# A feed-forward pipeline's token shift, moved to another place in GpSimd's order

## The chip, the cores and the metric

The kernel runs on one core of a Trainium2 chip. The metric is the device time of one execution in microseconds (us), the median of the runs shown. The engines are TensorE (PE in the profile), VectorE (DVE), ScalarE (ACT), GpSimd (POOL) and the DMA queues; each works through its own list of instructions in order, and they meet only at semaphores.

## The reference, cut to what matters

The whole program runs two blocks on 16 sequences of 256 tokens, 128 wide: a linear attention, a mixture of experts, a retention layer, and last a stack of two layers of local attention and a gated feed-forward part. The change touches only the feed-forward parts of those two layers:

```python
def shift_token(t):
    t1, t2 = jnp.split(t, 2, axis=-1)
    t2 = jnp.pad(t2, ((0, 0), (1, 0), (0, 0)))[:, :-1]
    return jnp.concatenate([t1, t2], axis=-1)

# in _layer, after the attention:
h = shift_token(x)
mu = h.mean(-1, keepdims=True)
var = h.var(-1, keepdims=True)
h = (h - mu) / jnp.sqrt(var + 1e-05) * lg + lb
h = h @ w1 + b1                       # 128 -> 2 x 341
a, g = jnp.split(h, 2, axis=-1)
h = a * jax.nn.gelu(g, approximate=False)
x = x + h @ w2 + b2                   # 341 -> 128
```

The shift takes the second half of the features from the token before, within each sequence.

## The kernel before, in words

The 4096 tokens are 8 chunks of 512 columns (`CH`), with the 128 features on the partitions. The feed-forward part works on pairs of chunks (`W = 2`, `PAIRS = 4`); within a pair the chunks are i = 0 and i = 1. The 341 hidden units are three blocks (`NHB`), j = 0, 1, 2, of 128, 128 and 85 rows. Each of the two layers has one such part, and a layer's part starts when the attention before it is done and ends before the next one's work.

One chunk goes through this chain:

1. GpSimd copies the chunk into `hs[i]` (`hsf` in the profile), the first 64 rows as they are and the other 64 moved by one token (`shift`, lines 2172 and 2173).
2. TensorE multiplies by the matrix that subtracts the mean (`centre`, L2216); ScalarE squares (L2270); TensorE averages the squares (`variance`, L2224); ScalarE takes logarithm and exponential for 1/sqrt (`roots`, L2276 and L2278).
3. VectorE multiplies, scales, and rounds to a high part (`inputs`, L2322, L2324, L2327). GpSimd subtracts to make the low part (`low_inputs`, L2181).
4. TensorE makes both halves of the hidden units from three products high*high, low*high, high*low (`hidden_units`, L2236); ScalarE applies gelu (L2286); VectorE multiplies with the other half (`units`, L2333).
5. The high part of the units comes from VectorE for chunk 0 (L2341) and from ScalarE for chunk 1 (L2295), the low part from GpSimd, three blocks of each chunk (`low_units`, L2190).
6. TensorE makes the output, nine matmuls for a chunk (`output`, L2248), and VectorE adds it to the residual stream `k.H` (L2346).

There is no planner: every engine has a loop over steps written by hand, and its order is the order of its queue. In a step s, TensorE works on three pairs at once:

```python
for step in range(PAIRS + 2):
    if step < PAIRS:
        centre(step)
    if step > 1:
        output(step - 2, 0)
    if step < PAIRS:
        variance(step)
    if step > 1:
        output(step - 2, 1)
    if 0 < step <= PAIRS:
        hidden_units(step - 1)
```

`centre(pair)` waits for each chunk's shift by the semaphore `shifted`. `output(pair, i)` waits for all low units of its chunk by `u_lo`. `hidden_units` waits for `hn_lo`. ScalarE loads the table for logarithm and exponential, does the squares and roots of pair s, loads the gelu table and does the gelus of pair s - 1. VectorE does the residual of pair s - 2 around the inputs of pair s, and then the units of pair s - 1.

GpSimd shifts pair 0 before its loop. In step s it then shifts pair s + 1, makes the low inputs of pair s, and the low units of pair s - 1. The shift has one pair of buffers `hs[0]`, `hs[1]`, which `centre` must have read before they are written again.

Of the kernel before, what the change touches and what calls it, by code (L numbers as in the profile page):

```python
# [8 lines left out]
F32 = mybir.dt.float32  # L9
BF16 = mybir.dt.bfloat16  # L10
F32R = mybir.dt.float32r
ALU = mybir.AluOpType
# [39 lines left out]
def hid_rows(j):  # L52
    return min(P, HID - j * P)


NHB = (HID + P - 1) // P
# [1590 lines left out]
def later(a):  # L1647

    return a.rearrange("p (s t) -> p s t", t=SEQ)[:, :, 1:SEQ]


def shifted_views(k, cols):

    return k.H[0:DH, cols], k.H[DH:P, cols].rearrange("p (s t) -> p s t", t=SEQ)[:, :, 0:SEQ - 1]
# [20 lines left out]
def local_layer(k, l, shared):  # L1675
# [4 lines left out]
    nc, ps = k.nc, k.ps  # L1680
    with ExitStack() as big:
# [5 lines left out]
        with ExitStack() as ctx:  # L1687
# [8 lines left out]
            W = k.sb(f"W{l}", [P, RING, CH], ctx=ctx)  # L1696
# [36 lines left out]
            @block.sync  # L1733
            def _(sp):
                for n in names:
                    sp.dma_start(w[n][:], k.dram[n][l]).then_inc(w_in, 16)
                if raw:
                    prepare_loads(k, l + 1, raw, sp)
# [404 lines left out]
        with ExitStack() as ctx:  # L2143
            W = 2
            PAIRS = NCH // W
# [3 lines left out]
            U = k.sb(f"Uf{l}", [P, W, NHB, CH], ctx=ctx)  # L2149
            U_parts = [k.sb(f"Uf_{part}{l}", [P, W, NHB, CH], F32R, ctx) for part in ("hi", "lo")]  # L2150
# [7 lines left out]
            first = lambda pair: G0 + W * pair  # L2158
            block = ctx.enter_context(nc.Block())

            @block.gpsimd
            def _(pool):

                def shift(pair):
                    if pair > 1:
                        pool.wait_ge(hn_lo, first(pair - 1))
                    for i in range(W):
                        c = first(pair) + i
                        early, late = shifted_views(k, here(c))
                        if pair > 0:  # L2170
                            pool.wait_ge(centred, c - 1)
                        nc.gpsimd.tensor_copy(hs[i][0:DH, :], early).then_inc(shifted, 1)
                        nc.gpsimd.tensor_copy(later(hs[i][DH:P, :]), late).then_inc(shifted, 1)
                    pool.wait_ge(shifted, 2 * (c + 1) + W * L)

                def low_inputs(pair):
                    for i in range(W):
                        c = first(pair) + i
                        hi, lo = (part[i] for part in hn_parts[pair % 2])
                        pool.wait_ge(hn_hi, c + 1)  # L2180
                        nc.gpsimd.tensor_tensor(lo[:], hn[i][:], hi[:].bitcast(F32), ALU.subtract).then_inc(hn_lo, 1)  # L2181

                def low_units(pair):
                    for i in range(W):
                        for j in range(NHB):
                            n = hid_rows(j)
                            if j == 0 and (i or pair):
                                pool.wait_ge(u_lo, NHB * (first(pair) + i))
                            pool.wait_ge((u_hi_dve, u_hi_act)[i], NHB * (first(pair) // W) + j + 1)
                            nc.gpsimd.tensor_tensor(U_parts[1][0:n, i, j, :], U[0:n, i, j, :],  # L2190
                                                    U_parts[0][0:n, i, j, :].bitcast(F32), ALU.subtract).then_inc(u_lo, 1)

                for i in range(W):
                    nc.gpsimd.memset(hs[i][:], 0.0).then_inc(shifted, 1)
                pool.wait_ge(shifted, 2 * G0 + W * L)
                shift(0)
                for step in range(PAIRS + 1):
                    if step > 1:
                        pool.wait_ge(u_lo, NHB * first(step - 1))
                    if step + 1 < PAIRS:  # L2200
                        shift(step + 1)
                    if step < PAIRS:
                        low_inputs(step)
                    if step > 0:
                        low_units(step - 1)

            @block.tensor
            def _(pe):
# [286 lines left out]
```

## Time and profile before

| | |
|---|---|
| time, median of 3 runs | 1434.64 us (1432.21 to 1435.32) |
| the profiled execution's own time | 1433.24 us |
| its span, first to last instruction | 1431.4 us |
| PE busy | 1210.3 us (85%) |
| DVE busy | 1043.1 us (73%) |
| ACT busy | 883.9 us (62%) |
| POOL busy | 844.3 us (59%) |
| mean granted TensorE clock | 0.941 of full |

The two feed-forward parts lie at about 970 to 1053 us and 1336 to 1420 us of the span. A timeline gives for each entry the start, the length, the engine, the line, the output and inputs by their names in the program, and in square brackets how long the engine had been idle before it and on what it had waited. A merged entry (x4) has the length of the whole group. A matmul of 32-bit floats with 512 columns shows as two entries of one line, so the two chunks of `centre` are an entry of x4. Entries of matmuls overlap their successors, because their ends are modelled.

### The profile page before, as it was taken

The numbers are of one execution on the slowest core, as the hardware profiler recorded it, in microseconds if no ns is written. First come the engines' busy times: TensorE is split into PE (matmuls) and PEld (weight loads), VectorE is DVE, ScalarE is ACT, GpSimd is POOL, SyncE is SP. The second block draws the span as 40 slices with busy tenths as digits, with TensorE's granted clock in tenths as the row PEclk, the third lists the DMA queues.
The fourth block names the chain that finished last, engine by engine and source line by source line (L and its number), as shares of the span: only waits on it lengthen the run. The fifth ranks groups of instructions, "written<-read, shape, count | busy, mean of one in ns | idle before, by whom it ended". The sixth has DMA issues, their size and how long they took to land. (4 is left out here: it accounts for less than half of the span.)

```text
span 1431.4 us, 26528 instructions
## 1 busy us (share of the span) xinstructions
PE 1210.3 (85%) x7852; PEld 787.8 (55%) x7852; DVE 1043.1 (73%) x2573; ACT 883.9 (62%) x2302; POOL 844.3 (59%) x778
## 2 busy tenths in 40 slices
PE   6879999963869997597699999966968999999796
PEld 3333344323548885242477777753645777777464
DVE  1289998975888996465688888843648888887464
ACT  6623333322536663176599899955648889899564
POOL 0054444505753667411688888877558887887663
PEclk9899999985989999699899999998979999999999
DMA  4800000002330221400100000000000000000001
GB/s 113 280 1 0 0 0 1 0 1 81 106 113 27 89 70 37 150 1 2 52 2 3 1 0 1 0 1 0 1 23 2 3 3 1 1 0 1 1 1 59
DMA packets 35021, 43.99 MB, mean 31 GB/s; under 512 B 5620, under 2 KB 24977, under 8 KB 34912
## 3 DMA queue, kind: packets, MB, share of 16 engines
q1 hardware_dynamic: 30304, 34.27, 7.5%
q0 software_dynamic: 4608, 8.47, 1.9%
q8 instruction: 43, 0.70, 0.2%
q14 instruction: 66, 0.54, 0.1%
HBM read 22.65 MB, written 21.12 MB: 31 GB/s over the span
## 5 line engine op out<-in xcount | busy, mean ns | idle before, releaser
L2066 DVE TENSOR_TENSOR R<-bank,tab 128x1024 f32<-128x1024 f32 x128 | 156.1, 1224 | 78.1 <-ACT sq L1976 77.1
L2010 ACT ACTIVATE W<-W,nm 128x128 f32<-128x128 f32 x512 | 198.2, 393 | 0.4
L1763 POOL TENSOR_TENSOR R<-R 128x512 f32<-128x512 f32 x128 | 161.3, 1282 | 15.1 <-DVE R L2066 15.1
L1778 POOL TENSOR_TENSOR W<-W,rden 128x512 f32<-128x512 f32 x128 | 132.8, 1040 | 50.5 <-DVE rden L2096 45.5
L2089 DVE CUSTOM_DVE_ANT_0 W<-bank,mask_q,rn 128x128 f32<-128x128 f32 x512 | 147.4, 344 | 17.7 <-PE bank L1878 13.1
L1308 POOL DMA_INDIRECT expert_rows<-Yt,xin x80 | 82.5, 1032 | 68.0 <-DVE Yt L1281 50.0
L1011 POOL DMA_INDIRECT expert_slots<-tok_rows,dst x64 | 67.2, 1050 | 65.9 <-ACT tok_rows L1035 45.1
L2010 ACT ACTIVATION_READ_ACCUMULATOR W<-W,nm 128x1 f32 x512 | 98.7, 193 | 0.0
L1994 ACT ACTIVATE QK<-bank 128x512 f32<-128x512 f32 x128 | 74.9, 586 | 35.2 <-PE bank L1853 33.5
L726 DVE TENSOR_TENSOR_SCAN S<-beta,U 128x512 f32<-128x512 f32 x64 | 93.5, 1482 | 0.0
L1903 PE MATMUL bank<-PT,VA 128*64 128x128 f32 (+1 forms) x1024 | 86.2, 262 | 3.7 <-ACT PT L2018 2.8
L1878 PE MATMUL bank<-QK 64*64 64x128 f32 x2048 | 86.3, 284 | 3.3 <-DVE nm L2089 3.0
L1976 ACT ACTIVATE sq<-bank 128x512 f32<-128x512 f32 x128 | 74.5, 582 | 19.0 <-PE bank L1832 18.3
L1772 POOL TENSOR_TENSOR R<-R,rn 128x512 f32<-128x512 f32 x64 | 66.7, 1042 | 28.9 <-ACT rn L1984 25.4
L1832 PE MATMUL bank<-wqkv_hi,hs_hi 128*128 128x512 f32 x128 | 64.2, 501 | 18.2 <-POOL hs_lo L1751 12.7
L2018 ACT ACTIVATE PT<-bank 128x512 f32<-128x512 f32 x128 | 74.8, 589 | 6.6 <-PE bank L1888 6.6
L2190 POOL TENSOR_TENSOR Uf_lo<-Uf,Uf_hi 128x512 fp32r<-128x512 f32 (+1 forms) x48 | 61.1, 1285 | 26.9 <-DVE Uf_hi L2341 26.2
L2073 DVE TENSOR_REDUCE sums<-sq 128x16 f32<-128x1024 f32 x64 | 76.8, 1201 | 0.0
L1888 PE MATMUL bank<-ident,W 128*128 128x128 f32 x512 | 75.7, 273 | 0.0
L1903 PEld LDWEIGHTS bank<-PT,VA 128*64 128x64 f32 x1024 | 52.2, 138 | 40.9 <-issue 40.8
L1888 PEld LDWEIGHTS bank<-ident,W 128*128 128x128 f32 x512 | 62.6, 140 | 15.9 <-issue 0.7
L1878 PEld LDWEIGHTS bank<-QK 64*64 64x64 f32 x2048 | 55.4, 133 | 20.9 <-issue 16.9
(350 smaller groups left out, 3475.9 us busy)
## 6 DMA issues: line engine op xcount, KB each, us to landing
expert_slots<-empty SPq DMA_DIRECT2D x8, 650.0 KB, 6.5
xin<-expert_slots SPq DMA_DIRECT2D x8, 650.0 KB, 6.1
expert_rows<-empty SPq DMA_DIRECT2D x8, 512.0 KB, 6.7
pair_rows<-expert_rows SPq DMA_DIRECT2D x16, 256.0 KB, 4.5
expert_raw<-w1e_dram SPq DMA_DIRECT2D x9, 256.0 KB, 2.9
expert_raw<-w2e_dram SPq DMA_DIRECT2D x9, 256.0 KB, 3.1
tok<-x_dram SPq DMA_DIRECT2D x8, 256.0 KB, 4.7
out_dram<-tok_out SPq DMA_DIRECT2D x8, 256.0 KB, 3.2
```

The source lines that it names most:

```text
L726: nc.vector.tensor_tensor_scan(S[i][:], beta[i % 2][:, chunk(c)], U[i // 2][:], 0.0, ALU.mult, ALU.add).then_inc(s_scan, 1)
L1308: nc.gpsimd.indirect_dma_start(k.ys[:, :], bass.IndirectOffsetOnAxis(ap=ids, axis=0), Yt[:, s % 3, t, :], None, bounds_check=2 * T - 1, oo ...
L1763: nc.gpsimd.tensor_tensor(halves[:, :, 0, :, z, :], halves[:, :, 0, :, z, :], halves[:, :, 1, :, 1 - z, :], ALU.add).then_inc(summed, 1)
L1778: nc.gpsimd.tensor_tensor(x, x, scale.to_broadcast([P, 4, P]), ALU.mult).then_inc(scaled, 1)
L1878: m = nc.tensor.matmul(ps[BS[i]][r:r + WIN, blk // 2 * P:(blk // 2 + 1) * P], QK[par][rows, b, o:o + WIN], keys, start=True, stop=True)
L1888: m = nc.tensor.transpose(ps[BT[p % 2]][:, a * P:(a + 1) * P], W[:, p % RING, a * P:(a + 1) * P], k.const["ident"][:])
L1903: m = nc.tensor.matmul(ps[BO[p % 2]][i * DH:(i + 1) * DH, cols], v[:, 2 * b + i, :], PT[:, p % 2, i * SEQ + cols.start:i * SEQ + cols.stop ...
L1994: nc.scalar.activation(QK[par][:, qk * NB:(qk + 1) * NB, t * P:(t + 1) * P], ps[BX[(t + 1) % 2]][:].rearrange("p (a b) -> p a b", a=NB), A ...
L2010: m = nc.scalar.activation(x, x, ACT.Exp, scale=-1.0, bias=nm[:, p % RING, j:j + 1], accum_out=den[:, p % RING, j:j + 1])
L2066: nc.vector.tensor_tensor(R[:, i, qk, :, :].rearrange("p c (h d) -> p c h d", d=DH), x, y.to_broadcast([P, 2, HEADS, DH]), ALU.mult).then_ ...
L2073: nc.vector.tensor_reduce(sums[:, i, :, 0:1].rearrange("p h o -> p (h o)"), sq[:].rearrange("p q (h d) -> p (q h) d", d=DH), AX.X, ALU.add ...
L2089: m = nc.vector.tensor_tensor_reduce(W[:, p % RING, j * P:(j + 1) * P], ps[BS[i]][:, cols], k.const["mask_q"][:, cols], rn[:, par, 2 * s + ...
```

## The change

GpSimd's order within a step is altered. `low_units` does one chunk at a time; the shift of the next pair no longer opens the step, but stands between the low units of the two chunks. In step 0, in which there are no low units, it follows the low inputs. Its waits on GpSimd's own earlier work (`hn_lo`, `u_lo`) are set to the new place. No instruction is added or taken away apart from waits, and the other engines' code is the same.

```diff
                 def shift(pair):
+                    if pair > 0:
+                        pool.wait_ge(hn_lo, first(pair))
                     if pair > 1:
-                        pool.wait_ge(hn_lo, first(pair - 1))
+                        pool.wait_ge(u_lo, NHB * (first(pair - 2) + 1))
                     for i in range(W):
...
-                def low_units(pair):
-                    for i in range(W):
-                        for j in range(NHB):
-                            n = hid_rows(j)
-                            if j == 0 and (i or pair):
-                                pool.wait_ge(u_lo, NHB * (first(pair) + i))
-                            pool.wait_ge((u_hi_dve, u_hi_act)[i], NHB * (first(pair) // W) + j + 1)
-                            nc.gpsimd.tensor_tensor(...).then_inc(u_lo, 1)
+                def low_units(pair, i):
+                    for j in range(NHB):
+                        n = hid_rows(j)
+                        if j == 0 and (i or pair):
+                            pool.wait_ge(u_lo, NHB * (first(pair) + i))
+                        pool.wait_ge((u_hi_dve, u_hi_act)[i], NHB * (first(pair) // W) + j + 1)
+                        nc.gpsimd.tensor_tensor(...).then_inc(u_lo, 1)
...
                 for step in range(PAIRS + 1):
                     if step > 1:
                         pool.wait_ge(u_lo, NHB * first(step - 1))
-                    if step + 1 < PAIRS:
-                        shift(step + 1)
                     if step < PAIRS:
                         low_inputs(step)
                     if step > 0:
-                        low_units(step - 1)
+                        low_units(step - 1, 0)
+                    if step + 1 < PAIRS:
+                        shift(step + 1)
+                    if step > 0:
+                        low_units(step - 1, 1)
```

## Rows read from the trace of the kernel before

**Rows 1.** Busy time in the two feed-forward parts; columns: engines, clock, DMA share, GB/s.

```profile
970.00:1053.00 83.00, 69.51 (x248) 44.41 (x248) 44.53 (x69) 48.53 (x69) 51.80 (x50) 0.96 0.00 1
1336.00:1420.00 84.00, 70.16 (x248) 44.43 (x248) 44.51 (x68) 48.42 (x68) 51.92 (x51) 0.96 0.00 1
```

**Rows 2.** Waits in the first layer's part: total us, times, longest.

```profile
PE bank L2248 <- POOL Uf_lo L2190: 3.7, 4, 1.5
```

**Rows 3.** Timeline of GpSimd in the first layer's part.

```profile
971.73 0.61 POOL L2173 COPY hsf<-H 64x510 f32<-64x510 f32 x1
...
974.60 0.61 POOL L2172 COPY hsf<-H 64x512 f32<-64x512 f32 x1 [0.94 <-PE bank L2216]
...
982.64 1.27 POOL L2181 TENSOR_TENSOR hnf_lo<-hnf,hnf_hi 128x512 fp32r<-128x512 f32 x1 [0.82 <-PE bank L2216]
983.98 0.60 POOL L2172 COPY hsf<-H 64x512 f32<-64x512 f32 x1
...
987.29 1.29 POOL L2181 TENSOR_TENSOR hnf_lo<-hnf,hnf_hi 128x512 fp32r<-128x512 f32 x1 [0.43 <-DVE hnf_hi L2327]
...
994.59 5.14 POOL L2190 TENSOR_TENSOR Uf_lo<-Uf,Uf_hi 85x512 fp32r<-85x512 f32 x4 [0.36 <-DVE Uf_hi L2341]
999.80 0.60 POOL L2172 COPY hsf<-H 64x512 f32<-64x512 f32 x1
...
1001.80 0.61 POOL L2173 COPY hsf<-H 64x510 f32<-64x510 f32 x1
1003.83 1.29 POOL L2181 TENSOR_TENSOR hnf_lo<-hnf,hnf_hi 128x512 fp32r<-128x512 f32 x1 [1.42 <-DVE hnf_hi L2327]
...
1012.05 5.12 POOL L2190 TENSOR_TENSOR Uf_lo<-Uf,Uf_hi 85x512 fp32r<-85x512 f32 x4 [0.36 <-DVE Uf_hi L2341]
```

**Rows 4.** Timeline of TensorE and ScalarE in the same part.

```profile
972.39 3.78 PE L2216 MATMUL bank<-hsf,centre 128*128 128x512 f32 x4 [13.68 <-POOL hsf L2173]
...
978.12 1.10 PE L2224 MATMUL bank<-sqf,mean 128*128 128x512 f32 x2 [0.87 <-ACT rsf L2276]
...
979.51 1.10 PE L2216 MATMUL bank<-hsf,centre 128*128 128x512 f32 x2 [0.29 <-DVE hnf L2322]
...
982.57 1.12 PE L2224 MATMUL bank<-sqf,mean 128*128 128x512 f32 x2
...
984.56 1.10 PE L2224 MATMUL bank<-sqf,mean 128*128 128x512 f32 x2 [0.87 <-ACT rsf L2276]
...
995.70 1.88 PE L2216 MATMUL bank<-hsf,centre 128*128 128x512 f32 x4
...
997.01 0.80 PE L2248 MATMUL bank<-Uf_hi,w2f_hi 128*128 128x512 f32 x1
...
998.71 1.09 ACT L2270 ACTIVATE sqf<-bank 128x512 f32<-128x512 f32 x2
...
999.51 1.02 PE L2224 MATMUL bank<-sqf,mean 128*128 128x512 f32 x2
...
1012.90 1.88 PE L2216 MATMUL bank<-hsf,centre 128*128 128x512 f32 x4
```

**Rows 5.** Timeline of TensorE at the next attention's start and the second layer's part.

```profile
1057.49 0.79 PE L1832 MATMUL bank<-wqkv_hi,hs_hi 128*128 128x512 f32 x1 [5.67 <-POOL hs_lo L1751]
...
1338.99 3.78 PE L2216 MATMUL bank<-hsf,centre 128*128 128x512 f32 x4 [3.75 <-POOL hsf L2173]
...
1345.35 1.10 PE L2224 MATMUL bank<-sqf,mean 128*128 128x512 f32 x2 [0.87 <-ACT rsf L2276]
```

**Rows 6.** Stretches after those two idle times, columns as in rows 1.

```profile
1055.00:1060.00 5.00, 2.51 (x6) 1.82 (x6) 0.20 (x1) 1.06 (x2) 2.31 (x2) 0.50 0.27 102
1338.00:1345.00 7.00, 5.49 (x6) 1.77 (x6) 0.00 (x0) 1.68 (x3) 4.53 (x8) 0.52 0.00 0
```

**Rows 7.** Timeline of VectorE: the same operation beside an idle and a busy GpSimd.

```profile
979.40 0.55 DVE L2324 TENSOR_SCALAR hnf<-hnf,vec 128x512 f32<-128x512 f32 x1
...
987.81 1.05 DVE L2324 TENSOR_SCALAR hnf<-hnf,vec 128x512 f32<-128x512 f32 x1
```

More of the change, by code:

```diff
@@ L2181, in low_inputs @@
                         nc.gpsimd.tensor_tensor(lo[:], hn[i][:], hi[:].bitcast(F32), ALU.subtract).then_inc(hn_lo, 1)
-                def low_units(pair):
-                    for i in range(W):
-                        for j in range(NHB):
-                            n = hid_rows(j)
-                            if j == 0 and (i or pair):
-                                pool.wait_ge(u_lo, NHB * (first(pair) + i))
-                            pool.wait_ge((u_hi_dve, u_hi_act)[i], NHB * (first(pair) // W) + j + 1)
-                            nc.gpsimd.tensor_tensor(U_parts[1][0:n, i, j, :], U[0:n, i, j, :],
-                                                    U_parts[0][0:n, i, j, :].bitcast(F32), ALU.subtract).then_inc(u_lo, 1)
+                def low_units(pair, i):
[4 more added lines that the diff above has]
+                        pool.wait_ge((u_hi_dve, u_hi_act)[i], NHB * (first(pair) // W) + j + 1)
+                        nc.gpsimd.tensor_tensor(U_parts[1][0:n, i, j, :], U[0:n, i, j, :],
+                                                U_parts[0][0:n, i, j, :].bitcast(F32), ALU.subtract).then_inc(u_lo, 1)
                 for i in range(W):
```

## The prediction, made before the changed kernel ran

> **What bounds the kernel now.** I read the page first. Its chain of work that ended last covers only the final output and says nothing of the stage that changes, so the answer must come from that stage. The busy times by window show two feed-forward parts of 83 and 84 us, TensorE busy 69.5 and 70.2 us of them, GpSimd only 51.8 [rows 1]. TensorE is the engine nearest to the bound, and in program order it holds the dependency chain of all three pairs in flight. Each part is a serial stretch: the attention before it must be done, and the next one needs its residual. So a microsecond lost on TensorE's order there is lost from the run.
>
> The list of waits shows TensorE waiting for GpSimd's low units four times, 3.7 us in all [rows 2]; those are in the last steps, where no shift stands in the queue, so the change cannot take them away. What matters is the timeline of GpSimd around each shift, beside TensorE's time of first use.
>
> - The shift of pair 1 is made at 974.60, as soon as `centre` has released the buffers, in a stretch in which GpSimd has nothing else to do until the first low inputs [rows 3]. TensorE uses it at 979.51, when its bank comes free [rows 4].
> - The shift of pair 2 starts at 983.98. After it GpSimd is still idle for 0.43 us until the high inputs of pair 1 come from VectorE [rows 3].
> - The shift of pair 3 starts at 999.80, and 1.42 us of idle time follow it, again until high inputs come [rows 3].
>
> So none of the three shifts delays the low inputs behind it: each lies in idle time. And each is ready long before TensorE wants it: `centre` of pair 2 runs at 995.70, that of pair 3 at 1012.90, both with no wait [rows 4]. A shift that costs nothing now can only be moved to a place where it costs something or nothing.
>
> **The change part by part.** A shift is four copies: from the start of the first (999.80) to the start of the fourth (1001.80) are 2.00 us, so one copy each 0.67, the first chunk ready after 0.67 + 0.61 = 1.28 and the second after 2.61 [rows 3]. TensorE starts 0.05 us after a shift is ready (971.73 + 0.61 = 972.34, then 972.39) [rows 3, 4]. GpSimd goes from one operation to a dependent one in 0.07 (982.64 + 1.27 = 983.91, then 983.98); that row already is a shift behind low inputs with a wait on the engine's own semaphore, so the altered waits on `hn_lo` and `u_lo` add nothing [rows 3].
>
> *Step 0, pair 1's shift.* There are no low units yet, so it stands behind the low inputs of pair 0, which end at 983.91 because they need the whole chain of pair 0. It starts at 983.98 instead of 974.60, and TensorE starts `centre` of chunk 0 at 983.98 + 1.28 + 0.05 = 985.31 instead of 979.51, of chunk 1 at 986.64. Queued behind `centre` on TensorE are `variance` of pair 1 and then all hidden units of pair 0, whose inputs have long been ready. What counts is when the second `variance` starts, for hidden units follow it at once; before, that is 984.56 [rows 4]. At full clock: an entry of four matmuls takes 1.88, four passes of about 0.43, so TensorE can start the first `variance` 0.87 after the second `centre`, at 987.51; the second follows 1.99 later (982.57 to 984.56) [rows 4], at 989.50. That is 4.9 us late.
>
> TensorE's last work before is at 978.12 + 1.10 = 979.22 [rows 4], so it would now stand idle for 6.1 us. The trace has two near rows: after 5.67 us of idle time the granted clock is 0.50 (1.2 GHz), and after 3.75 us it is 0.52 in the next 7 us [rows 5, 6]. With half clock the same sequence, two `centre` and two `variance` whose shifts arrive 1.3 us apart, can be read at the two starts: from first `centre` to second `variance` 978.12 - 972.39 = 5.73 us in layer 0 and 1345.35 - 1338.99 = 6.36 us in layer 1 [rows 4, 5]. Then the second `variance` is at 985.31 + 5.73 to 6.36 = 991.0 to 991.7, which is 6.5 to 7.1 us late. I take 6.8, the middle, for the idle times of 3.75 and 5.67 us are shorter than 6.1 and still ended in half clock [rows 5, 6], and after the longer one, 13.68 us, four matmuls took 3.78 us instead of 1.88 [rows 4].
>
> The Trainium skill, in "TensorE: Matmul & The Clock Gate", section on HAM oscillation, says that a pause of TensorE between bursts makes the next burst start at half rate, and that this is paid at each such pause. By that rule step 0 costs 6.8 us; with the clock kept it would cost 4.9. The rows agree with the rule.
>
> *Step 1, pair 2's shift.* From here on all is late by the same amount, so I reckon with the old times. The last low units of chunk 0 start at 994.59; the entry of four takes 5.14, one 1.285 [rows 3]. They end at 995.88, the shift starts at 995.95, and `centre` runs its chunk 0 at 997.28 and chunk 1 at 995.95 + 2.61 + 0.05 = 998.61. Before, chunk 1 ran two passes after 995.70, at 996.57 [rows 4]. So TensorE is 2.05 us late behind it. ScalarE does not cover this: its squares start at 998.71 because of the table load [rows 4], but between `centre` and `variance` TensorE has the nine matmuls of `output` (997.01 to 999.51) [rows 4], which start behind chunk 1's `centre` and run gapless into `variance`. All 2.05 us reach `variance`, and from there roots, inputs and the hidden units of pair 1.
>
> *Step 1, low units of chunk 1.* They are behind the shift, so they end at 995.88 + 2.65 + 3 * 1.285 = 1002.4 instead of 999.73. The `output` that needs them starts at about 999.51 + 2.05 + 2.4 = 1004.0, so nothing waits. GpSimd is free for pair 2's low inputs at 1002.5, and these come at 1003.83 + 2.05. Cost nothing; the cover is 1.6 us on TensorE's side.
>
> *Step 2, pair 3's shift.* The same with 1012.05: ready for chunk 1 at 1012.05 + 1.285 + 0.07 + 2.61 + 0.05 = 1016.07 instead of 1012.90 + 0.87 = 1013.77 [rows 3, 4]. 2.30 us late.
>
> *Steps 3 and 4* have no shift and keep their lengths.
>
> *What is gained.* While GpSimd copies, a VectorE operation of pair 1 takes 1.05 us instead of 0.55 [rows 7]. That shift is no longer beside it. But gelu is needed by the next VectorE work at nearly the same time, so I take 0 and at most 0.5 us a part. The Trainium skill, "GPSIMD Engine Reference", section on specifications, says that the two engines share their interfaces to SBUF and get in each other's way; the rows agree, and by it alone this change would save that half microsecond.
>
> *The sum.* Per layer 6.8 + 2.05 + 2.3 = 11.15 us, for both 22.3. Layer 1's part has the same order and the same length [rows 1]. 1433.24 + 22.3 = 1455.5 us. The profiled execution was 1.4 below the median of the runs; half of that is within their scatter, so I say 1456.
>
> **The rivals.**
>
> *A. The clock does not fall.* Layers cost 4.9 + 2.05 + 2.3 = 9.25 each: 1433.24 + 18.5 = 1451.7. Against it stand the three idle times above.
>
> *B. The clock stays low through hidden units.* The attention after 1057.49 is still at 0.50 well into its matmuls [rows 6]. Pair 0's first twelve hidden matmuls would then take double: nine gapless ones take 2.50 us (997.01 to 999.51) [rows 4], so twelve take 3.3 and would take 3.3 more, part of it beside the load of the gelu table. In both layers up to 1433.24 + 22.3 + 6.6 = 1462.1, and 1458.8 if half of it shows.
>
> *C. No change.* The late shifts would have to be hidden by TensorE's own waits. For it: TensorE waits 0.87 us for ScalarE ahead of each second `variance` [rows 4]. Against: those waits follow the late work and move with it. Time 1434.
>
> *D. Faster.* The shift at the head of steps 1 and 2 holds GpSimd for 2.7 us ahead of low inputs. If these were the real bound, through a wait that the profile puts elsewhere, four shifts (two a layer) would give 4 * 2.7 = 10.8: 1422.4. It decides only if low inputs became ready before the shift was over; the idle 0.43 and 1.42 us behind the shifts say that they did not [rows 3].
>
> **How the numbers follow.** Forecast 0.66, A 0.12, B 0.14, C 0.05, D 0.03. Bounds within the forecast: clock rows 6.47 and 7.10, the gain of 0 to 0.5 a part, the scatter of the runs of 1.5: 1453 to 1458. With A and B the range is 1450 to 1461. What can be told from no change is 0.2%, 2.9 us: slower 0.92, same 0.05, faster 0.03.
>
> **What the profile after would show.** GpSimd's timeline: in step 0 low inputs first, then copies; TensorE idle about 6 us before the second pair's `centre`, put down to the copy L2173; a granted clock of 0.5 right after; waits on L2173 of about 1.5 and 0.5 us before `centre` of pair 2, and 1.8 and 0.5 before that of pair 3; parts of about 94 and 95 us; everything outside them as before. The prediction is wrong if the first `variance` of pair 1 is not late, or if the parts keep 83 us.

## The result, and the profile after

The changed kernel takes 1457.85 us (median of 4 runs, 1456.21 to 1462.35), the kernel before 1434.98 us in the same comparison (1432.21 to 1437.57): ratio 1.0163, 95% interval 1.0143 to 1.0182. It is slower by 22.9 us; the forecast was 1456.0 us, range 1450 to 1461.

The profiled execution of the changed kernel took 1457.24 us, its span is 1455.4 us, 24.0 more than before. Busy times of VectorE, ScalarE and GpSimd are those of before within 1.2 us. TensorE has 7.7 us more with the same 7852 matmuls. All of it lies in the two feed-forward parts (72.4 and 75.0 us instead of 69.5 and 70.2), where the granted clock is 0.93 and 0.89 instead of 0.96 [rows 1]: the same work, more of it at the lower clock. The busy times of the whole execution:

```profile
PE 1218.0 (84%) x7852; PEld 790.3 (54%) x7852; DVE 1043.4 (72%) x2573; ACT 884.7 (61%) x2302; POOL 843.1 (58%) x778
```

The list of waits of the first feed-forward part has the one group that grew on TensorE: it waits for the shift's second copy (now L2175) 23.4 us in six waits, where before it did so once, for 13.7 us, at the part's start. The waits for low units are the same 3.7 us as in [rows 2]:

```profile
PE bank L2219 <- POOL hsf L2175: 23.4, 6, 13.7
...
PE bank L2251 <- POOL Uf_lo L2191: 3.7, 4, 1.5
```

GpSimd's timeline shows the three shifts in their new places, in answer to [rows 3]. The first stands behind the low inputs of pair 0, with 7.21 us of idle time behind it; the other two, of which the first is shown, stand behind the third low unit of chunk 0, with the three of chunk 1 right behind them:

```profile
982.85 1.26 POOL L2183 TENSOR_TENSOR hnf_lo<-hnf,hnf_hi 128x512 fp32r<-128x512 f32 x1 [0.82 <-DVE hnf_hi L2330]
984.18 0.60 POOL L2174 COPY hsf<-H 64x512 f32<-64x512 f32 x1
...
986.17 0.61 POOL L2175 COPY hsf<-H 64x510 f32<-64x510 f32 x1
993.99 1.29 POOL L2183 TENSOR_TENSOR hnf_lo<-hnf,hnf_hi 128x512 fp32r<-128x512 f32 x1 [7.21 <-DVE hnf_hi L2330]
...
1001.52 1.29 POOL L2191 TENSOR_TENSOR Uf_lo<-Uf,Uf_hi 85x512 fp32r<-85x512 f32 x1 [0.36 <-DVE Uf_hi L2344]
1002.93 0.60 POOL L2174 COPY hsf<-H 64x512 f32<-64x512 f32 x1
...
1004.92 0.61 POOL L2175 COPY hsf<-H 64x510 f32<-64x510 f32 x1
1005.62 3.76 POOL L2191 TENSOR_TENSOR Uf_lo<-Uf,Uf_hi 128x512 fp32r<-128x512 f32 x3
1012.97 1.29 POOL L2183 TENSOR_TENSOR hnf_lo<-hnf,hnf_hi 128x512 fp32r<-128x512 f32 x1 [3.60 <-DVE hnf_hi L2330]
```

TensorE's timeline, in answer to [rows 4]: `centre` (now L2219) waits 6.08 us in step 1 of TensorE, 1.47 + 0.21 in the next, 1.71 + 0.21 in the one after. The rows from 1005.59 to 1008.65 show how `output` and the first `variance` follow the second `centre` without a gap, so a late `centre` is a late `variance`:

```profile
978.33 1.10 PE L2227 MATMUL bank<-sqf,mean 128*128 128x512 f32 x2 [0.87 <-ACT rsf L2279]
985.50 3.78 PE L2219 MATMUL bank<-hsf,centre 128*128 128x512 f32 x4 [6.08 <-POOL hsf L2175]
989.08 1.62 PE L2227 MATMUL bank<-sqf,mean 128*128 128x512 f32 x2
991.56 1.10 PE L2227 MATMUL bank<-sqf,mean 128*128 128x512 f32 x2 [0.87 <-ACT rsf L2279]
...
1004.26 1.12 PE L2219 MATMUL bank<-hsf,centre 128*128 128x512 f32 x2 [1.47 <-POOL hsf L2175]
1005.59 1.12 PE L2219 MATMUL bank<-hsf,centre 128*128 128x512 f32 x2 [0.21 <-POOL hsf L2175]
1006.15 0.80 PE L2251 MATMUL bank<-Uf_hi,w2f_hi 128*128 128x512 f32 x1
...
1008.65 1.02 PE L2227 MATMUL bank<-sqf,mean 128*128 128x512 f32 x2
...
1023.93 1.13 PE L2219 MATMUL bank<-hsf,centre 128*128 128x512 f32 x2 [1.71 <-POOL hsf L2175]
```

The busy times by window of the same stretch: in the idle stretch TensorE does nothing, and in the 6.5 us behind it the granted clock is 0.63 on average, that is, mostly the 1.2 GHz level. The matmuls of 985.50 took 3.78 us, the same as the cold four in [rows 4].

```profile
979.50:985.40 5.90, 0.00 (x0) 0.00 (x0) 2.90 (x6) 2.56 (x3) 3.69 (x4) 0.83 0.00 1
985.50:992.00 6.50, 5.63 (x7) 2.05 (x8) 0.00 (x0) 2.43 (x4) 1.22 (x2) 0.63 0.00 0
```

**Where the time went, part by part.** The start of the first part moves by several us from run to run for reasons outside it, so the experiments below are read by the parts' own lengths in the profiled execution: from the start of the first copy of the shift to the start of the last residual on VectorE.

| kernel | first part, us | second part, us | more than before |
|---|---|---|---|
| before | 80.79 | 81.47 | |
| changed | 92.10 | 94.67 | 11.31 + 13.20 |
| e1_step0_back | 85.33 | 87.66 | 4.54 + 6.19 |
| e2_only_step0 | 88.13 | 88.45 | 7.34 + 6.98 |
| e3_kept_busy | 90.71 | 90.95 | 9.92 + 9.48 |
| e4_shift_last | 96.77 | 96.06 | 15.98 + 14.59 |
| e5_after_low_inputs | 80.78 | 81.63 | -0.01 + 0.16 |
| e6_last_low_on_dve | 80.19 | 80.96 | -0.60 - 0.51 |
| e7_and_short_clear | 80.91 | 80.00 | 0.12 - 1.47 |
| e8_prepare_in_gaps | 80.97 | 81.51 | 0.18 + 0.04 |
| e9_and_short_clear | 81.42 | 80.50 | 0.63 - 0.97 |

The two parts are 24.5 us longer where the whole span is 24.0 us longer, so the rest of the program is 0.5 us shorter.

A part's length also scatters by up to 0.9 us for a reason at its start, where TensorE comes out of idle time at half clock. From the first copy to the first low input it takes between 9.2 and 10.1 us, whatever the kernel. In the second part it is 10.12 us in every run but e7 and e9, where it is 9.2; in e7 the granted clock of the first 7 us is 0.76, before it was 0.52 [rows 6]. So 0.9 of the 1.5 us by which e7's second part is shorter is this scatter.

### The profile page after: what moved, and what is told of

Read it like the earlier page. It is cut to its first block and busy times, and to the rows that moved or that the text cites. A ratio compares the mean times of both kernels' runs of the same rounds, so it can differ in the third digit from the quotient of the medians.

```text
span 1455.4 us, 26528 instructions
## 1 busy us (share of the span) xinstructions
PE 1218.0 (84%) x7852; PEld 790.3 (54%) x7852; DVE 1043.4 (72%) x2573; ACT 884.7 (61%) x2302; POOL 843.1 (58%) x778
```

## The experiments

The theory (L) is that TensorE's `centre` waits for each late shift, and everything behind it in TensorE's order is late by as much. The rivals are U, that the low units of chunk 1, which now stand behind a shift, are what costs; and K, that it is mostly the clock that falls in the first wait. Where an experiment moves a shift, the waits at the head of `shift` are set to the new place; these lines are left out of the diffs below.

**e1_step0_back** undoes the move in step 0 alone:

```diff
 for step in range(PAIRS + 1):
+    if step == 0:
+        shift(1)
     if step < PAIRS:
         low_inputs(step)
     if step > 0:
         low_units(step - 1, 0)
-    if step + 1 < PAIRS:
+    if 0 < step and step + 1 < PAIRS:
         shift(step + 1)
```

> Pair 1's shift is made ahead of pair 0's low inputs again, as before; the shifts of pairs 2 and 3 stay between the low units. Theory L (TensorE's centre waits for each late shift): only step 0's part of the loss goes, 6.6 us in layer 0 and 7.0 in layer 1 of the changed kernel's trace, so 1457.9 - 13.7 = 1444, which is about 9 to 11 us slower than before. Rival U (the loss comes from chunk 1's low units, which stand behind the shift): step 0 has no low units, so the time stays at 1457 to 1458. Rival K (the loss is mostly TensorE's half clock after its 6 us idle time): near 1437.

Measured: 1447.92 us against 1434.21 before on the same chip, ratio 1.0083 (1.0051 to 1.0115). The median is 4 us above the expectation. In the profiled execution the parts lengthened by 10.7 us together, as expected (9 to 11); that run's first part started at 976.66 instead of 971.07, an excess that lies ahead of the change. In this experiment and the next three, the medians differ from the kernel before by 2.3 to 3.0 us more than the parts do. Why is open; the profiled executions of e2 and e4 start their first part late too (975.58 and 975.96), that of e3 hardly (971.71). U expected no difference from the changed kernel, and K 1437, a loss of 2 to 3 us: by the times and by the parts both fell. TensorE still waits as before for pair 2:

```profile
1002.75 1.12 PE L2220 MATMUL bank<-hsf,centre 128*128 128x512 f32 x2 [1.46 <-POOL hsf L2174]
1004.08 1.13 PE L2220 MATMUL bank<-hsf,centre 128*128 128x512 f32 x2 [0.21 <-POOL hsf L2174]
```

**e2_only_step0** makes the move in step 0 alone:

```diff
 for step in range(PAIRS + 1):
+    if 0 < step and step + 1 < PAIRS:
+        shift(step + 1)
     if step < PAIRS:
         low_inputs(step)
-    if step > 0:
-        low_units(step - 1, 0)
-    if step + 1 < PAIRS:
-        shift(step + 1)
-    if step > 0:
-        low_units(step - 1, 1)
+    if step == 0:
+        shift(1)
+    if step > 0:
+        low_units(step - 1, 0)
+        low_units(step - 1, 1)
```

> Only pair 1's shift is moved behind pair 0's low inputs; the shifts of pairs 2 and 3 open their steps as before. Theory L: before plus 13.7 us, about 1448 to 1449. Rival U: same as before, 1435. Rival K: about 1457.

Measured: 1450.86 us, ratio 1.0107 (1.0077 to 1.0137). The parts grew by 7.34 and 6.98, 14.3 against the 13.7 expected. U expected 1435 and K 1457; both fell again. With e1 the two halves of the change add up: 4.54 + 7.34 = 11.88 in the first part (11.31 together), 6.19 + 6.98 = 13.17 in the second (13.20). The row of the wait, the same 6.08 us:

```profile
990.17 3.78 PE L2220 MATMUL bank<-hsf,centre 128*128 128x512 f32 x4 [6.08 <-POOL hsf L2175]
```

**e3_kept_busy** gives TensorE matmuls to do in that wait; their results are overwritten and not used:

```diff
 for step in range(PAIRS + 2):
+    if step == 1:
+        for _ in range(6):
+            nc.tensor.matmul(ps[BO][:], k.const["mean"][:], sq[0][:], start=True, stop=True)
     if step < PAIRS:
         centre(step)
```

> The changed kernel, with six more matmuls on TensorE (their results are overwritten and used by nobody) ahead of pair 1's centre, so that it is busy for about 5 of the 6 us in which it waits for that shift. Theory L: the wait itself stays, the granted clock after it stays at full, and step 0 costs 4.9 us a layer instead of 6.6 and 7.0, so 1457.9 - 3.9 = 1454. Rival K: at least 10 us back, 1448 or less. Rival U: no change from 1458.

Measured: 1456.57 us (1453.16 to 1460.27), ratio 1.0156 (1.0118 to 1.0193). By the times alone this cannot be told from the changed kernel. By the parts it can: they grew by 9.92 and 9.48 instead of 11.31 and 13.20, 5.1 us back where 3.9 were expected. About 1.5 of it is a second fall of the clock that the changed kernel's profile has in its second part (below) and this one has not. The added matmuls, the `centre` behind them, which still waits for the shift, and the granted clock of the 8 and 9 us around them:

```profile
980.03 5.31 PE L2258 MATMUL bank<-sqf,mean 128*128 128x512 f32 x12
986.28 1.13 PE L2219 MATMUL bank<-hsf,centre 128*128 128x512 f32 x2 [0.94 <-POOL hsf L2175]
```

```profile
979.00:987.00 8.00, 6.97 (x16) 2.87 (x16) 3.53 (x6) 3.21 (x4) 4.41 (x6) 1.00 0.00 1
987.00:996.00 9.00, 6.42 (x20) 3.36 (x20) 4.47 (x8) 6.38 (x9) 2.84 (x3) 1.00 0.00 0
```

With the clock kept, what stays, 9.9 and 9.5, is the waits alone; K fell. Step 0 by itself is read from a part's first low input to its third low unit, which leaves out the scatter at the start. In the kernel before it is 994.59 - 980.55 = 14.04 us, with the row of 994.59 in [rows 3] and

```profile
980.55 1.26 POOL L2181 TENSOR_TENSOR hnf_lo<-hnf,hnf_hi 128x512 fp32r<-128x512 f32 x1 [3.04 <-DVE hnf_hi L2327]
```

Here it is 1000.44 - 981.53 = 18.91 us, 4.87 more, and in the second part 4.86 more:

```profile
981.53 1.27 POOL L2183 TENSOR_TENSOR hnf_lo<-hnf,hnf_hi 128x512 fp32r<-128x512 f32 x1 [7.22 <-DVE hnf_hi L2333]
...
1000.44 1.30 POOL L2191 TENSOR_TENSOR Uf_lo<-Uf,Uf_hi 85x512 fp32r<-85x512 f32 x1 [0.36 <-DVE Uf_hi L2347]
```

**e4_shift_last** keeps pair 1's shift where it was and puts the other two behind all low units:

```diff
     if step > 0:
         low_units(step - 1, 0)
+        low_units(step - 1, 1)
-    if step + 1 < PAIRS:
+    if 0 < step and step + 1 < PAIRS:
         shift(step + 1)
-    if step > 0:
-        low_units(step - 1, 1)
```

> Pair 1's shift as before; the shifts of pairs 2 and 3 come last in their steps, behind all low units. Theory L: centre of chunk 1 is ready 5.9 us late in step 1 and 6.1 in step 2, 24 us in two layers, so 1459, and up to 1467 if the clock falls in each of the four waits of about 5 us. Rival U: the low units are not held back by any shift, so the time is that of before, 1435.

Measured: 1467.72 us, ratio 1.0226 (1.0196 to 1.0257), at the upper end of L's range and the slowest of all, with low units in the order and at the place of before. U is dead: it expected 1435. The parts grew by 16.0 and 14.6, where 12 each were expected from the waits at full clock; the clock fell at each of the four waits of 5.3 to 5.5 us. The first of them and the clock in and behind it:

```profile
1005.83 3.78 PE L2219 MATMUL bank<-hsf,centre 128*128 128x512 f32 x4 [5.26 <-POOL hsf L2174]
```

```profile
1000.00:1005.80 5.80, 0.57 (x3) 0.10 (x1) 0.80 (x2) 3.02 (x4) 5.52 (x6) 0.93 0.00 0
1005.80:1012.00 6.20, 6.17 (x11) 3.52 (x12) 0.00 (x0) 1.19 (x2) 1.22 (x2) 0.51 0.00 0
```

**e5_after_low_inputs** is the counterpart: GpSimd makes the low units of the first two pairs later than before, but no shift is late for TensorE.

```diff
     if step < PAIRS:
         low_inputs(step)
+    if 0 < step and step + 1 < PAIRS:
+        shift(step + 1)
     if step > 0:
         low_units(step - 1, 0)
-    if step + 1 < PAIRS:
-        shift(step + 1)
-    if step > 0:
-        low_units(step - 1, 1)
+        low_units(step - 1, 1)
```

> Pair 1's shift as before; the shifts of pairs 2 and 3 stand behind the low inputs and ahead of all low units of their step, so GpSimd makes every low unit later than before (by up to 2.3 us for chunk 0), but each shift is ready before TensorE's centre wants it. Theory L: nothing but the first output is touched, 0.3 us in step 1 (low units of chunk 0 end at 997.3, TensorE could start at 997.0): no change, the parts stay at 80.8 and 81.5 us to within 1 us, the time within 1434 to 1436. Rival U (late low units are what costs): at least 2 us in each of the four steps, parts of 85 and more, 1442 or more.

This and the next two ran on another chip, on which the kernel before takes 1491.71 us; the difference lies ahead of the feed-forward parts, so their lengths can be compared. Measured: 1493.16 us, ratio 1.0010 (0.9995 to 1.0024), no difference, and parts of 80.78 and 81.63. `centre` of pair 2 runs without a wait, and the six low units are one entry behind the shift:

```profile
1056.24 1.88 PE L2218 MATMUL bank<-hsf,centre 128*128 128x512 f32 x4
```

```profile
1053.31 0.69 POOL L2173 COPY hsf<-H 64x510 f32<-64x510 f32 x1
1054.09 7.81 POOL L2189 TENSOR_TENSOR Uf_lo<-Uf,Uf_hi 128x512 fp32r<-128x512 f32 x6
```

Counted from the part's start, the first low unit of pair 0 is 2.2 us late (22.19 instead of 19.98) and its last ends 1.3 us late (30.00 instead of 28.66), and the parts are at most 0.2 us longer for it, while in the changed kernel a shift that is 2 us late costs 2 us. This alone doesn't clear the low units of chunk 1, which in the changed kernel stand 2.7 us further behind those of chunk 0 than before; e4 and the unchanged 3.7 us of waits for low units do.

**e6_last_low_on_dve** goes after the longest of the four waits of [rows 2], on the kernel before. VectorE makes the last pair's low units of chunk 1. GpSimd leaves them out, and TensorE's last `output` waits for the new semaphore; that is not shown:

```diff
 # VectorE, in the last step, with a semaphore of its own
+    dve.wait_ge(u_hi_act, NHB * (first(PAIRS - 1) // W) + j + 1)
+    nc.vector.tensor_tensor(U_parts[1][0:n, 1, j, :], U[0:n, 1, j, :],
+                            U_parts[0][0:n, 1, j, :].bitcast(F32), ALU.subtract).then_inc(u_lo_dve, 1)
 ...
```

> The kernel before, with the last pair's three low units of chunk 1 made by VectorE, which has nothing to do there, no longer by GpSimd behind chunk 0's. Before, TensorE waits 1.48 us for them between its last two outputs in each part. Theory: those waits go, a part is 1.5 us shorter (79.3 and 80.0), the time 3 us or 0.2% less, about 1431. Rival: VectorE's operations stand in its queue ahead of chunk 0's residual and push that back, so nothing is won.

Measured: 1493.73 us, ratio 1.0011 (0.9998 to 1.0024): nothing. The parts are 0.6 and 0.5 us shorter, not 1.5. The wait did not go but got shorter and changed its releaser: `output` also needs the residual of chunk 0, because the two share a bank. That residual was not pushed back by VectorE's new work, as the rival had it: it starts 76.95 us after the part's start, where it was 76.96. In the kernel before it ended at 1048.78 and the wait for the low units at 1049.47, so there was never more than about 0.6 us to win.

```profile
1109.07 0.47 PE L2257 MATMUL bank<-Uf_hi,w2f_hi 128*128 128x512 f32 x1 [1.00 <-DVE H L2361]
```

**e7_and_short_clear** adds to that a shorter clearing of the shift buffers at the part's start:

```diff
-    nc.gpsimd.memset(hs[i][:], 0.0).then_inc(shifted, 1)
+    nc.gpsimd.memset(hs[i][DH:P, :].rearrange("p (s t) -> p s t", t=SEQ)[:, :, 0:1], 0.0).then_inc(shifted, 1)
```

> The one before, and the clearing of the shift buffers at a part's start touches only the two columns of the upper rows that no copy writes, not all 512 columns of both buffers. Before, the two clearings take 0.99 us ahead of the first shift, with TensorE waiting. Theory: about 0.8 us less in a part, another 1.6 us in all, 1429 to 1430. Rival: an operation of GpSimd has a fixed cost near its time for 512 columns, so nothing changes.

Measured: 1491.34 us, ratio 0.9991 (0.9978 to 1.0004): not told from no change. Against e6, on which it is built, it is 2.4 us less, where 1.6 were expected. The first copy comes 0.20 us after the first clearing, where it was 1.06, so the 0.8 us a part are there, ahead of the stretch that the table measures:

```profile
1030.28 0.13 POOL L2195 MEMSET hsf<- 64x2 f32 x2 [0.55 <-POOLq L1687]
1030.48 0.60 POOL L2173 COPY hsf<-H 64x512 f32<-64x512 f32 x1
```

**e8_prepare_in_gaps** takes the lesson the other way round: find GpSimd's work for which TensorE does wait, and put it where GpSimd is idle. Of TensorE's 13.68 us of idle time before the first part [rows 4], 10.3 us go to preparing the second layer's weights and tables: from the first of these operations at 959.68 to the clearing of the shift buffers at 970.01. The buffers of the raw weights must live longer for it, and the waits for them move along; that is not shown.

```diff
 # GpSimd, at the end of the first layer's attention
-    prepare_split(k, l + 1, raw, pool)
 # GpSimd, in the feed-forward loop, behind the shift and ahead of the low inputs
+    if raw and step == PAIRS - 1:
+        split_quarter(k, l + 1, raw, pool, 0)
+    if raw and step == PAIRS:
+        split_quarter(k, l + 1, raw, pool, 1)
+        split_quarter(k, l + 1, raw, pool, 2)
+        scale_tables(k, raw)
 ...
```

> The kernel before, with GpSimd's preparation of the second layer's weights and tables (L1411, L1414, L1417, 10.3 us at the end of the first layer's attention, while TensorE stands idle for 13.7 us) made inside the first feed-forward part, where GpSimd waits anyway: a third of the weights in step 3 (3.85 us of idle time, needs 2.8), the rest in step 4 (6.6 us of idle time, needs 7.0). Theory L's view that only what TensorE waits for counts: the idle time before the first part falls from 13.7 to about 3.7 us, the part itself stays near 81 us (at most 1 us longer, for VectorE's operations beside GpSimd's and 0.4 us of overhang), so 9 to 10 us or 0.65% less. Rival: GpSimd's added work in the part pushes low inputs and low units back and eats it: 0.2% or less.

Measured: 1424.90 us against 1434.11 before on that chip, ratio 0.9937 (0.9923 to 0.9950): 9.2 us less. TensorE's idle time before the first `centre` is 3.74 us, the parts are 80.97 and 81.51, and low inputs of pair 3 still find GpSimd waiting 0.86 us for them. TensorE's idle time is 9.9 us shorter, of which 0.5 is given back: from its first low input on, the first part is 0.5 us longer, and so much later do its last low units end behind the added work:

```profile
965.08 1.71 PE L2239 MATMUL bank<-hsf,centre 128*128 128x512 f32 x2 [3.74 <-POOL hsf L2187]
```

```profile
1011.22 1.28 POOL L1410 TENSOR_TENSOR wqkv_lo<-wqkv_raw,wqkv_hi 128x512 fp32r<-128x512 f32 x1
1013.37 1.29 POOL L2195 TENSOR_TENSOR hnf_lo<-hnf,hnf_hi 128x512 fp32r<-128x512 f32 x1 [0.86 <-DVE hnf_hi L2350]
```

**e9_and_short_clear** has e7's shorter clearing on top of that, without e6's edit.

> The one before, and the clearing of the shift buffers only in the two columns that no copy writes. By the profile of the kernel with that edit a part begins 0.8 us earlier (clearings 0.2 instead of 1.05 us ahead of the first copy), so 1.7 us or 0.1% less than without it, 0.75% less than the kernel before. Rival: the scatter of the runs hides it.

Measured: 1423.72 us, ratio 0.9933 (0.9919 to 0.9946). It is the fastest of all, 0.7% under the kernel before; the 1.2 us to e8 are within the scatter.

## Why the prediction was right

*That each shift lay in idle time and could only lose by moving.* Right. With shifts off the head of the step nothing got faster: e5 moves two of them from ahead of the low inputs to behind them, by 6.2 and 7.5 us, and changes nothing.

*Step 0, 6.8 us.* Measured by the third low unit of pair 0: 994.59 before and 1001.52 after, 6.93 later, of which 0.29 was there at the part's start: 6.64. In the second part 7.02. Both lie within the 6.5 to 7.1 that the two cold starts had given. The start of `centre` was forecast for 985.31 and came at 985.50, which with the 0.29 is 0.1 early.

*The clock, 1.9 of these 6.8.* Right, and shown by e3: the idle time was 6.08 and 6.07 us in the two parts, the clock fell in both, and with the clock kept step 0 costs 4.87 and 4.86 us, as forecast (4.9). Measured in the same way, from the first low input on, it costs 6.72 and 7.02 in the changed kernel, so the clock's share is 1.9 and 2.2 us.

*Step 1, 2.05 us, and step 2, 2.30 us.* Measured 2.21 and 2.48. From the third low unit to the next low inputs it is 1012.97 - 1001.52 = 11.45, before 1003.83 - 994.59 = 9.24 [rows 3], hence 2.21. Of the missing 0.16, 0.1 is the start of `output`: it comes 0.56 us after chunk 1's `centre` when TensorE has just waited, and about 0.45 when it runs gapless. The rest is the start of the copies, 0.12 us after the low unit and not 0.07.

*The waits as forecast.* The first wait of each pair came as forecast, 1.47 and 1.71 us for 1.5 and 1.8. The second was forecast at 0.5 and is 0.21. That is no other mechanism: the two chunks start 1.33 us apart as forecast (1004.26, 1005.59), and the profile counts the first chunk's matmuls as busy for 1.12 us, where two passes of 0.43 make 0.87.

*Step 2 of the second part, 4.0 instead of 2.3 us.* This term was too small. The forecast had clock falls only in step 0. In this execution the clock also fell at the 1.9 us of waits there, 1.5 us more, so the second part grew by 13.2 and not 11.15; e1's profile has the same one and e3's has not. Whether it falls in so short a wait differs from run to run, and the kernel before has no wait there to fall in.

*Low units of chunk 1 behind the shift cost nothing.* Right: the waits for them are the same 3.7 us, and e5 and e4 say the same from both sides.

*The gain beside VectorE.* The operation of [rows 7] takes 0.76 instead of 1.05 us. The forecast took 0 to 0.5 us a part for it, and it is near 0: in e4, where pair 1's shift is as before and pair 2's is out of VectorE's way, the low inputs of pair 1 in the second part come 0.36 us earlier after the part's start, and the third low unit 0.07.

*The rivals.* A (clock kept) is what e3 had to make by hand. B did not happen: the granted clock was full from the first hidden unit of pair 0 on, in the first part

```profile
992.10:995.50 3.40, 3.38 (x14) 2.23 (x12) 3.05 (x5) 2.74 (x4) 1.29 (x1) 1.00 0.00 0
```

and likewise in the second, from 1370.10. C and D fell with the waits themselves.

*The sum.* It was 22.3 us; 24.5 were lost in the parts and 0.5 won outside. The medians differ by 22.9. The mechanism is what the forecast said, step by step; that the medians come within 0.6 us of the sum is in part luck, since the second fall of the clock, 1.5 us of the profiled execution, was not in it.

## What to carry to other kernels

Ask of every operation in a helper engine's queue by when its reader wants it, not how much idle time stands beside it. The shift's reader stands at the head of the busiest engine's step, so at the head of the helper's step, where it looked like an obstacle, it lay in idle time and cost nothing; in steps 1 and 2 it could stand behind the low inputs at no cost (e5), in step 0 it could not (e2). Wherever it came too late for TensorE, that cost what it was late, and the fall of the clock on top. Then look for the helper work that the busy engine does wait for: ten microseconds of weight preparation fitted into those same idle stretches. A wait on two semaphores is listed under one name; before taking the named one away, reckon when the other is ready (e6).

## What the runs showed of the hardware

Idle times of TensorE of 5.3 to 6.1 us each ended in half clock, eight of eight in the changed kernel, e2 and e4. Waits of only 1.7 + 0.21 us were followed by it in the second part of the changed kernel and of e1, and not in the first part of either nor in e3. That the wait caused it is not shown; no part without such a wait had a fall at this place. Here are that wait and the matmul behind it, at half speed (2.08 instead of 1.12 us):

```profile
1402.03 1.13 PE L2219 MATMUL bank<-hsf,centre 128*128 128x512 f32 x2 [1.71 <-POOL hsf L2175]
1403.36 2.08 PE L2219 MATMUL bank<-hsf,centre 128*128 128x512 f32 x2 [0.21 <-POOL hsf L2175]
```

Six matmuls whose results nobody reads kept the clock full (1.00 instead of 0.63 behind the wait) and gave back about 2 us each time, though `centre` still started only when its shift was there.

The same kernel took 1434 us on one chip and 1492 us on another. The difference lies ahead of the first feed-forward part, which starts at 1031.90 in e5 and at 971.07 in the kernel before on the other chip; the cause is open.
